# Expert blocks of a graph layer: rows gathered in quarters of columns and transposed by VectorE in 32x32 pieces

## The reference

```python
h = layernorm(x)                         # x: rows after the two other parts
scores = maximum(h @ gate_W + gate_b, 1e-4)          # 8 experts
p = softmax(scores);  two best experts per row
w = maximum(p, 0.1) / (sum of the two)
y = einsum('bsd,edf->bsef', h, expert_W) + expert_b  # expert_W: 8 x 1024 x 1024
x = x + sum over the two chosen experts of w * y / 2
```

## Time and profile before

| | us |
|---|---|
| median of 3 runs | 1191.75 |
| lowest, highest | 1190.89, 1193.56 |
| profiled execution, its own time | 1190.14 |
| its span, first to last instruction | 1188.3 |
| last stage, first matmul of a block to the last | 896.5 to 1176.9 |

### The profile page before, as it was taken

One profiled execution on the slowest core, in us unless ns is written; L12 is line 12 of the kernel. 1 busy time (PEld: TensorE's weight loads), 2 busy tenths in 40 slices (PEclk: granted clock), 3 DMA queues, 4 the chain that ended last, 5 costly groups with the idle time before them and its releaser, 6 DMA issues.

```text
span 1188.3 us, 15152 instructions
## 1 busy us (share of the span) xinstructions
PE 1148.8 (97%) x5588; PEld 984.9 (83%) x5588; DVE 587.7 (49%) x1171; ACT 308.7 (26%) x416; POOL 462.5 (39%) x394
## 2 busy tenths in 40 slices
PE   6999999999999999999999999999959999999996
PEld 5898888888788999999988878888847788788884
DVE  7935666555332122211133447997589622744444
ACT  2421212133111121211022213343353411623232
POOL 0003457457787577511000015233323444443433
PEclk9999999999999999999999999999968999999998
DMA  9382785783634444477457633463288954876653
GB/s 355 114 347 50 204 226 117 232 210 36 137 48 43 93 93 94 97 159 153 92 175 244 204 109 116 166 243 131 94 297 307 336 87 91 257 235 128 190 88 72
DMA packets 115835, 192.15 MB, mean 162 GB/s; under 512 B 33960, under 2 KB 63912, under 8 KB 114624
## 3 DMA queue, kind: packets, MB, share of 16 engines
q1 hardware_dynamic: 81008, 159.53, 39.0%
q0 software_dynamic: 34768, 31.82, 19.8%
HBM read 136.19 MB, written 61.68 MB: 167 GB/s over the span
## 4 chain that ended last, share of the span: by engine, by line
PE 89%; DVE 8%; issue 1%; ACT 1%; DMA 0%; DVEq 0%; POOL 0%; ACTq 0%; POOLq 0%
PE ps L1564 28%; PE ps L1565 28%; PE ps L1566 28%; DVE e_lo L1389 2%; PE ps L1783 2%; PE ps L1712 2%; PE ps L1652 2%; DVE xn_lo L1116 1%; DVE stats L1088 1%; DVE acc L1104 1%; PE ps L1610 1%; DVE y L1534 0%; ACT lt_hi L1012 0%; DMA acc<-in_x 0%; DVE tok_w L1503 0%
## 5 line engine op out<-in xcount | busy, mean ns | idle before, releaser
L734 POOL DMA_INDIRECT cnt_d<-times,addr_i x160 | 263.0, 1644 | 179.1 <-DMA cnt_d<-times,addr_i 96.0
L1564 PE MATMUL ps<-e_hi,lt_hi 128*128 128x512 f32 x368 | 148.0, 402 | 2.8 <-DVE e_lo L1389 2.3
L1566 PE MATMUL ps<-e_hi,lt_lo 128*128 128x512 f32 x368 | 144.1, 392 | 0.0
L1565 PE MATMUL ps<-e_lo,lt_hi 128*128 128x512 f32 x368 | 144.1, 391 | 0.0
L1565 PE MATMUL ps<-xt_lo,q_hi 128*128 128x416 f32 (+1 forms) x384 | 135.0, 352 | 0.0
L1564 PE MATMUL ps<-xt_hi,q_hi 128*128 128x416 f32 (+1 forms) x384 | 135.0, 351 | 0.0
L1566 PE MATMUL ps<-xt_hi,q_lo 128*128 128x416 f32 (+1 forms) x384 | 134.6, 351 | 0.0
L842 POOL DMA_INDIRECT out<-y,row_put x46 | 73.7, 1602 | 87.8 <-ACT y L1046 51.4
L1564 PEld LDWEIGHTS ps<-e_hi,lt_hi 128*128 128x128 f32 x368 | 69.6, 189 | 23.2 <-DVE e_lo L1389 9.0
L1257 DVE TENSOR_TENSOR qs<-ps,qs 128x416 f32<-128x416 f32 (+1 forms) x24 | 14.2, 592 | 136.9 <-PE ps L1566 136.9
L1566 PEld LDWEIGHTS ps<-e_hi,lt_lo 128*128 128x128 f32 x368 | 69.5, 189 | 14.9
(11 more groups left out here) (257 smaller groups left out, 2382.0 us busy)
## 6 DMA issues: line engine op xcount, KB each, us to landing
e_raw<-in_L_ffn_expert_W SPq DMA_DIRECT2D x64, 512.0 KB, 9.8
cnt_d<-zeros SPq DMA_DIRECT2D x20, 640.0 KB, 12.2
rows<-key_d SPq DMA_DIRECT2D x8, 1250.0 KB, 7.5
acc<-in_x SPq DMA_DIRECT2D x18, 512.0 KB, 7.5
w_raw<-in_L_mix_w_key SPq DMA_DIRECT2D x16, 512.0 KB, 4.4
cnt_d<-cnt_d POOLq DMA_DIRECT2D x10, 640.0 KB, 7.6
cnt<-cnt_d SPq DMA_DIRECT2D x10, 640.0 KB, 5.9
h_d<-hs SPq DMA_DIRECT2D x18, 256.0 KB, 2.3
```

What stands on the lines that cost most here:

```text
L734: nc.gpsimd.indirect_dma_start(out=cnt_d[i], out_offset=bass.IndirectOffsetOnAxis(ap=addr_i[:, j:j + 1], axis=0), in_=times[:, j:j + 1], i ...
L1564: nc.tensor.matmul(o, lh, rh, start=(k == 0), stop=False)
L1565: nc.tensor.matmul(o, lh, rl, start=False, stop=False)
L1566: return nc.tensor.matmul(o, ll, rh, start=False, stop=(k == last_k))
```

## The change

The gather of a block becomes four: gather t fetches, for all 128 partitions, 1 KB each into the columns 256t to 256t+255 of `gx`. Partition 32q+j gets the quarter q of the row that stands in slot 32t+j. If each 32x32 piece of that tile is then transposed in place, the whole is the transposed block, with the contraction in another order: partition 32q+i of the piece c holds the column 256q+32c+i. VectorE's transpose does that, two instructions of 128x512 into the banks 4 and 5. The weights are loaded in the matching order of rows: one DMA per quarter of the partitions and pair of row blocks. The first block is still gathered whole; ScalarE brings its columns into the new order (`gp`) and TensorE transposes it. The index table `quad_of` is made with four small matmuls by `sel`, a permuted identity, and one instruction of VectorE.

GpSimd's loop is in a new order: both waits for the scatters before and one copy of both row indices stand ahead of the four gathers. `AT_ONCE` goes from 3 to 2, and two row blocks of expert 2 are loaded after the first block is turned, since `gp` lies in their place.

```diff
-    AT_ONCE = 3
+    AT_ONCE = 2
+    QD = 32
+    NQD = P // QD
+    QK = D // NQD
...
             def load_expert(e, rows, running=None):
-                for k in rows:
+                for k in rows[::2]:
                     if running is not None and k == AT_ONCE:
-                        sp.wait_ge(s_gx, first_block[running] * 16 + 32)
+                        sp.wait_ge(s_gx, first_block[running] * 64 + 80)
                     b = e % NLO
-                    sp.dma_start(e_raw[b][k][:, :], expert_W[e, k * P:(k + 1) * P, :]).then_inc(s_er[b][k // 2], 16)
+                    for q in range(NQD):
+                        sp.dma_start(e_raw[b][k // 2][q * QD:(q + 1) * QD, :, :],
+                                     expert_W[e, q * QK + k * QD:q * QK + (k + 2) * QD, :].rearrange("(c i) n -> i c n", i=QD)
+                                     ).then_inc(s_er[b][k // 2], 16)
...
             sp.wait_ge(s_gx, 16)
-            load_expert(2, range(KB))
+            load_expert(2, range(KB - 2))
+            sp.wait_ge(s_tr, 2)
+            load_expert(2, range(KB - 2, KB))
...
+            def gather_quads(index):
+                for t in range(NQD):
+                    nc.gpsimd.indirect_dma_start(out=gx[:, t * QK:(t + 1) * QK], out_offset=None,
+                                                 in_=xn2_d.rearrange("n (b k) -> (n b) k", b=NQD),
+                                                 in_offset=bass.IndirectOffsetOnAxis(ap=index[t], axis=0)).then_inc(s_gx, 16)
...
             pool.wait_ge(s_tr, 2)
-            gather_rows(tok_of[:, 1:2])
+            pool.wait_ge(s_quad, 1)
+            gather_quads([quad_of[:, t, 1:2] for t in range(NQD)])
...
             with pool.Fori(0, blocks) as i:
                 pool.wait_ge(s_tr, i * 2 + 4)
-                nc.gpsimd.tensor_copy(tok_now[:, :], tok_of[:, bass.ds(i + 2, 1)]).then_inc(s_tok, 1)
+                nc.gpsimd.tensor_copy(tok_now[:, :, :], quad_of[:, :, bass.ds(i + 2, 1)]).then_inc(s_tok, 1)
+                for h in range(NH):
+                    pool.wait_ge(s_sc[h], i * 16 + 16)
+                    pool.sem_inc(s_passed, 1)
+                nc.gpsimd.tensor_copy(row_put[:, :, :], row_of[:, :, bass.ds(i, 1)]).then_inc(s_put, 1)
                 pool.wait_ge(s_tok, i + 1)
                 pool.sem_inc(s_passed, 1)
-                gather_rows(tok_now[:, :])
+                gather_quads([tok_now[:, t, :] for t in range(NQD)])
+                pool.wait_ge(s_put, i + 1)
+                pool.sem_inc(s_passed, 1)
                 for h in range(NH):
                     c = slice(h * HALF, (h + 1) * HALF)
-                    pool.wait_ge(s_sc[h], i * 16 + 16)
-                    pool.sem_inc(s_passed, 1)
-                    nc.gpsimd.tensor_copy(row_put[:, h:h + 1], row_of[:, h, bass.ds(i, 1)]).then_inc(s_put, 1)
-                    pool.wait_ge(s_put, i * 2 + (1 + h))
-                    pool.sem_inc(s_passed, 1)
                     pool.wait_ge(s_y[h], i + 2)
...
+            act.wait_ge(s_gx, 16)
+            for g in range(2):
+                nc.scalar.copy(gp[:, MB * g:MB * g + MB, :].rearrange("p c (q i) -> p c q i", q=NQD),
+                               gx[:, :].rearrange("p (q c i) -> p c q i", q=NQD, c=KB)[:, MB * g:MB * g + MB, :, :]).then_inc(s_gp, 1)
             for g in range(2):
                 block_hi(0, g)
...
+                if t == NT - 1:
+                    for q in range(NQD):
+                        V.tensor_copy(sel[:, :, q * QD:(q + 1) * QD], ident[:, :].rearrange("p (t j) -> p t j", t=NQD))
...
+            for q in range(NQD):
+                V.memset(quad[q * QD:(q + 1) * QD, :], float(q))
...
             V.tensor_scalar(slot_f[:, :], ps[:, 2, 0:NSLOT], -1.0, None, ALU.add)
+            V.tensor_scalar(tok_f[:, :], ps[:, 2, 0:NSLOT], -1.0, 0.0, ALU.add, ALU.max).then_inc(s_tokf, 1)
...
+            def block_turned(g):
+                V.transpose(ps[:, 4 + g, :].rearrange("p (c t j) -> p c t j", c=MB, t=NQD),
+                            gx[:, :].rearrange("p (t c i) -> p c t i", t=NQD, c=KB)[:, MB * g:MB * g + MB, :, :]).then_inc(s_tr, 1)
...
             last.then_inc(s_wtab, 1)
+            dve.wait_ge(s_quadp, 1)
+            V.tensor_scalar(quad_of[:, :, :], ps[:, 3, 0:NQD * NSLOT].rearrange("p (t s) -> p t s", t=NQD), float(NQD), quad[:, 0:1],
+                            ALU.mult, ALU.add).then_inc(s_quad, 1)
             dve.wait_ge(s_padt, 1)
...
                         V.tensor_tensor(yb[:, c], ps[:, h, :], bias[e % NBIAS][:, c], ALU.add).then_inc(s_ye, 1)
+                        if h == 0:
+                            dve.wait_ge(s_gx, i * 64 + 80)
+                            for g in range(2):
+                                block_turned(g)
...
-            pe.wait_ge(s_gx, 16)
             for g in range(2):
+                pe.wait_ge(s_gp, g + 1)
                 block_transposes(g)
+            pe.wait_ge(s_tokf, 1)
+            for t in range(NQD):
+                last = nc.tensor.matmul(ps[:, 3, t * NSLOT:(t + 1) * NSLOT],
+                                        sel[:, t, :], tok_f[:, :],
+                                        start=True, stop=True)
+            last.then_inc(s_quadp, 1)
...
-                        if h == 0:
-
-                            pe.wait_ge(s_gx, i * 16 + 32)
-                            pe.wait_ge(s_llo, i * 2 + 2)
-                            for b in range(2):
-                                block_transposes(b)
```

More of the change, by code:

```diff
@@ L169, in gps_layer @@
         e_lo = [[at(f"e_lo{b}_{k}", LO_AT[b][k], [P, D], f32r) for k in range(KB)] for b in range(NLO)]
-        e_raw = [[at(f"e_raw{b}_{k}", LO_AT[b][k], [P, D]) for k in range(KB)] for b in range(NLO)]
+        e_raw = [[at(f"e_raw{b}_{k}", LO_AT[b][k], [P, 2, D]) for k in range(0, KB, 2)] for b in range(NLO)]
+        assert all(LO_AT[b][k + 1] == LO_AT[b][k] + D for b in range(NLO) for k in range(0, KB, 2))
         assert BIG + 2 * KB * D + MB * D == A and MB * D == 4096
@@ L237, in gps_layer @@
         slot_f = gate("slot_f", [P, NSLOT])
-        slot_e = gate("slot_e", [P, NSLOT])
+        quad_of = gate("quad_of", [P, NQD, NSLOT], i32)
+        sel = at("sel", X + HALF, [P, NQD, P], f16)
+        gp = at("gp", RING + (2 * KB - 1) * D, [P, KB, P])
         row_of = at("row_of", RAW + 2 * NT * NE, [P, NH, NSLOT], i32)
@@ L275, in gps_layer @@
         last_c = at("last_c", EX + 3 * D, [P, NE, NSLOT], f16)
-        tok_now = small("tok_now", [P, 1], i32)
-        row_put = small("row_put", [P, NH], i32)
+        tok_now = small("tok_now", [P, NQD, 1], i32)
+        tok_f = small("tok_f", [P, NSLOT], f16)
+        quad = small("quad", [P, 1])
+        row_put = small("row_put", [P, NH, 1], i32)
         hexp = small("hexp", [P, 1])
@@ L842, in _ @@
                     nc.gpsimd.indirect_dma_start(out=out.rearrange("n (h c) -> (n h) c", h=NH),
-                                                 out_offset=bass.IndirectOffsetOnAxis(ap=row_put[:, h:h + 1], axis=0),
+                                                 out_offset=bass.IndirectOffsetOnAxis(ap=row_put[:, h, :], axis=0),
                                                  in_=y[:, c], in_offset=None, compute_op=ALU.add).then_inc(s_sc[h], 16)
-            pool.wait_ge(s_gx, blocks * 16 + 32)
+            pool.wait_ge(s_gx, blocks * 64 + 80)
             pool.sem_inc(s_passed, 1)
@@ L1005, in expert_hi @@
                 for k in rows:
-                    act.wait_ge(s_er[e % NLO][k // 2], 32 * (e // NLO + 1))
-                    nc.scalar.copy(e_hi[e % 2][:, k, :], e_raw[e % NLO][k][:, :]).then_inc(s_ehi, 1)
+                    act.wait_ge(s_er[e % NLO][k // 2], 16 * NQD * (e // NLO + 1))
+                    nc.scalar.copy(e_hi[e % 2][:, k, :], e_raw[e % NLO][k // 2][:, k % 2, :]).then_inc(s_ehi, 1)
             def block_hi(i, g):
@@ L1782, in block_transposes @@
                     k = MB * g + b
-                    last = nc.tensor.transpose(ps[:, 4 + g, b * P:(b + 1) * P], gx[:, k * P:(k + 1) * P], ident[:, :])
+                    last = nc.tensor.transpose(ps[:, 4 + g, b * P:(b + 1) * P],
+                                               gp[:, k, :], ident[:, :])
                 last.then_inc(s_tr, 1)
-            pe.wait_ge(s_gx, 16)
             for g in range(2):
+                pe.wait_ge(s_gp, g + 1)
                 block_transposes(g)
+            pe.wait_ge(s_tokf, 1)
[4 more added lines that the diff above has]
+            last.then_inc(s_quadp, 1)
             pe.wait_ge(s_wtab, 1)
```

3 lines of the change are left out of this document (2 added, 1 removed).

## The result

The changed kernel takes 1289.61 us, the median of 4 runs (1287.01 to 1290.72), beside 1191.74 for the kernel before: a ratio of 1.0816, 95% interval 1.0794 to 1.0838. The forecast was 1244 and its range ended at 1278. So it is slower, as forecast, and the ring that was forecast is there; but it is slower by 98 us instead of 52, and two further costs make up the difference. The profiled execution took 1287.01 us for a span of 1284.9; the forecast span was 1240.3, and the 44.6 us between these two are what the experiments have to explain.

The account below looks back on a forecast made before the run. TensorE bounded the kernel before; the change would make GpSimd's ring the bound. 919.8 + 22 turns x 13.5, + 15 under load, + 8.5 gave 1240.3 us of span, 1244 us as median of runs; range 1203 to 1278.

Parts of the forecast that it names:

- the ring: GpSimd's loop: scatter landing, four gathers, left scatter, right scatter; no block shorter than one turn, 13.5 us.
- Part 1: Expert blocks: eight transposes leave TensorE in each of 23 blocks, a gain of 20.0 us if nothing else grows.
- Part 2: VectorE gets two transposes per block at 0.69 us each, 1.4 us per block, hidden in undisturbed blocks.
- Part 3: GpSimd's loop: both scatter waits before four gathers make a 13.5 us turn the bound; +15 us under weight loads.
- the price of a gather: GpSimd's loop: 1.01 us per gather instruction, set by the instruction and its 128 rows, not by bytes.
- the dear end: Upper end of the turn, 14.5 us: 1.14 us per gather, the dearest of 23, and a landing of 5.3.
- Part 4: Other work per block is covered by the turn: TensorE has 2.6 us of slack, passes at expert starts (9.2) fit.
- Part 6: Weight loads in 256 KB pieces to 32 partitions stay hidden; a cited half-rate rule would add some 9 us.
- rival B: The ring binds and narrow loads run at half rate: +14, and +3 twice, 1264 us; chance 0.18.
- Part 5: Ahead of the blocks: first block starts 1.9 us late, first right scatter of the loop at 919.8.
- Part 7: The end: the span ends 8.5 us after the last right scatter starts, unchanged.
- Rival A: The ring doesn't bind, four gathers together under 2.4 us: 5.5 us faster, 1186 us; chance 0.15.

Follow-up runs that it names:

- a_order: The changed kernel with the four gathers moved ahead of the waits for the scatters, loads still narrow: 1225.46 us, ratio 1.029.
- a_one: The changed kernel with one gather of whole rows in place of each four, so the result is wrong: 1218.01 us, ratio 1.0221.
- m_wide_order: The changed kernel with 128-partition loads (rows 8p to 8p+7 per partition), transposes reading every eighth column, gathers ahead of the scatter waits: 1208.68 us.
- a_psum: The changed kernel, low-half passes of experts 1 to 7 reading their second operand from zeroed PSUM, so those low halves are left out: 1272.39 us.
- b_narrow: The kernel before with each 512 KB weight load split into four of 32 partitions, 128 KB each: 1203.15 us, ratio 1.0108.
- a_wide: The changed kernel with weights loaded 128 partitions at once in plain row order, so the result is wrong: 1272.39 us, ratio 1.0691.
- experiment 4: The changed kernel with wide loads that keep the result, in two runs: m_wide, 1279.09 us, and m_wide_order, 1208.68 us.
- m_wide: The changed kernel with 128-partition loads (rows 8p to 8p+7 per partition) and transposes reading every eighth column, GpSimd's order left: 1279.09 us.
- m_lo1: m_wide_order with VectorE's low-half passes reading one SBUF operand, times zero, so the low halves are left out: 1200.63 us, ratio 1.0069.
- w_wide_order: The changed kernel with 128-partition loads whose source is four stretches of 32 rows, and the gathers ahead of the scatter waits: 1331.88 us.

## Why the forecast was right and wrong

- **Part 1, transposes gone from TensorE: right.** TensorE's blocks are 10.88 us apart where nothing else binds (`a_order`, `a_one`, `m_wide_order`), for the 10.9 forecast and the 11.8 of the earlier trace rows.
- **Part 2, VectorE's transposes at 0.69 us: right.** Duration of one, least, median and most, then who waited for it:

```profile
L1521 DVE STREAM_TRANSPOSE ps<-gx x46: 682/706/729, 918.0 to 1264.6; 128x512 f32<-128x512 f32 x46
...
  ACT lt_hi L1034: 200.4, 20
```

- **Part 3, the ring: right in an undisturbed block,** 13.3 to 13.7 for 13.5, by 5.25 of landing for 4.8 and a gap of 0.69 ahead of the gathers and 0.30 behind them for 0.84 and 0.6. TensorE's share of the span is 90% for the 91% forecast. Taken back alone, the order of the waits is worth 64 us (`a_order`) and the three extra gathers 72 (`a_one`); each takes the ring off the path, so the two don't add up.
- **Part 3, the price of a gather, 1.01 us and at the dearest 1.14: wrong at the experts' starts.** This is one of the two steps that failed, and the one to which the forecast gave nothing. In the kernel before, the gather issued in an expert's first block lies right among VectorE's passes (second line of the fence below, while the passes of the earlier trace rows run from 1153.28 to 1162.4) and takes 1.14 us, little more than elsewhere; so 1.14 became the dear end. In the changed kernel four groups of the loop take about 1.64, 1.92, 1.92 and 1.97 us, 3.5 us more than elsewhere, and three more groups are long in part. Part 4 checked that the passes fit in time into the turn ("fit as well"), and they do. It did not ask what they do to the ring's own instructions. `a_psum` puts 17.2 us on this. GpSimd's timeline of the kernel before, and VectorE's around it:

```profile
1158.83 0.25 POOL L829 COPY tok_now<-tok_of 128x1 int32 x1 [2.89 <-PE ps L1783]
1159.92 1.14 POOL L808 DMA_INDIRECT gx<-xn_d,tok_now  x1 [0.84 <-POOL tok_now L829]
```

```profile
1158.96 2.35 DVE L1389 TENSOR_TENSOR e_lo<-e_raw,e_hi 128x1024 fp32r<-128x1024 f32 x2
```

  What set the price was where in a pass the gather fell. Passes start 1.14 us apart (those two at 1158.96 and 1160.1). In both kernels every gather of the loop that starts while a pass runs, with another pass behind it, ends 0.8 to 1.0 us after that next one starts, as if it had waited for the end of the running one. The gathers of the kernel before start 0.97 us into a pass, all six of them, and wait 0.17. In the changed kernel the first gather of five of the seven groups starts 0.48 into a pass and takes 1.64. The next one starts 0.30 behind its end, which is 0.16 into a fresh pass, and pays nearly the whole of it, and so does each that follows. The row of 1.14 us was a lucky moment, read as a bound.

- **Part 6, the loads hidden: wrong; rival B was partly right.** This is the other step that failed, worth as much. The loads run at about half rate. The rule of the Trainium skill, SBUF — State Buffer, "Door 1: The DMA port swizzle", cited there, agrees with the trace: it gives 189 GB/s, and the trace shows 207 to 238 with the other transfers counted. The narrow transfers are also smaller, 256 KB for 512 KB, and no run makes them smaller alone; but with the 128 KB of `b_narrow` the queue of the loads moves 10.8 MB in the 58 us from 918 on, and 11.2 MB with the 256 KB of the changed kernel, which speaks against the size. Part 6 priced this at 9 us and left it out of the sum, and rival B had 20 (14 for more loaded turns and 6 for the expert of one block), against the 17.2 of `a_wide`. Neither has the start in it: 7.5 of the 17.2 us lie ahead of the first right scatter, where expert 1's and 2's loads delay the first gathers. In the stretch from 918 to 976 a scatter lands 9.8 us after its issue (median of six), not 8.0.
- **Part 5, the start:** 931.5 for 919.8. With wide loads 924.0, with short gathers too 920.4. The steps were sound; both missing terms struck here as well. **Part 7:** 6.8 for 8.5.
- **Two sums in the working are off, without weight in the total.** Part 4 puts the last gather 3.8 us ahead of the right scatter; its own terms give 3.5 (1.01 + 0.6 + 1.59 + 0.30), the trace 3.2. Part 5 goes from 893.5, by half of 1.97, to 894.9; it is 894.5.
- **Rival A** fell as forecast for the kernel as written. Its arithmetic for a ring that does not bind, 1186 us, was too good as well: `m_wide_order` is such a kernel and takes 1208.7, if with transposes of 1.13 us. The experts' starts, priced at 1.9 us more each, cost more there, as experiment 4 shows.

What stays open: how the 8 us by which the two disturbances together exceed their single effects divide over the turns, and why `m_wide` is 6.7 us slower than `a_wide`; the strided transposes are a suspect, which no run took apart.

## What to carry to other kernels

When a change makes a chain of waits the bound, price every instruction on it where it will stand, beside whatever runs then, and not from rows in which it stood alone or fell at one fixed moment of its neighbour: a delay that was free off the path is paid in full on it. Count the semaphores' order in a queue as part of the change, for four gathers ahead of a wait instead of behind it were worth 64 us here. And read a rule that speaks against a change as a term with a size in every stage that uses the resource, the start included.

## What was not expected of the hardware

- An indirect gather issued by GpSimd takes 0.95 us, and behind another one 1.92 to 1.97 beside VectorE passes with both operands in SBUF; with one of them in PSUM and the same length of pass it takes 0.95. The Trainium skill, SBUF — State Buffer, "Who interferes with whom", says that an instruction of VectorE with two SBUF inputs contends with a GpSimd instruction that reads SBUF, and that one with at most one SBUF input does not, outside the modes in which it uses two ports. `a_psum` agrees, and shows that a gather's instruction counts as such a reader. The same section tells of a probe in which `tensor_tensor` did not stall a DMA; the gathers here are delayed beside it (1.92 us for 0.95), and for them the measurement decides. It names `tensor_scalar` among the instructions that can enter such a mode, and the passes of `m_lo1` are `tensor_scalar`, at 0.69 us for 1.15: the gathers of 1.19 to 1.59 us beside them would fit, which no run tests. The section was not used in the forecast, though it bore on the change.
- Loads of 512 KB over 128 partitions whose source is four separate stretches of rows ran at 103 to 107 GB/s with a DMA share of 0.2 (`w_wide_order`). The same rows in DMAs of 32 partitions ran at 207 and more.
- A VectorE transpose from SBUF to PSUM of 128x512 float32 takes 0.71 us with 32 columns in a row and 1.13 with a stride of eight (medians of 46).
